# Cross attention: square sums of the eight head pairs in one burst at the end of a block, in four column groups

## The chip, the core and the metric

One core of one Trainium2 chip runs the kernel as a single launch. The metric is device time in microseconds (us), median over the executions. A core has five engines that run their own instruction lists and meet at semaphores: TensorE (PE; its weight loads are listed as PEld), VectorE (DVE), ScalarE (ACT), GpSimd (POOL) and SyncE (SP), which here only starts DMAs. Matmul results land in PSUM, eight banks of 128 partitions x 512 float32.

## What is computed

The program is one decoder layer in float32: a gated delta attention, a cross attention over 77 context tokens, and a mixture of 8 experts. The change lies in the cross attention alone. In the terms of the reference (its set-up calls the pieces `L0_xattn`):

```python
# 4 sequences x 1024 tokens x 256; 16 heads of 64; context (4, 77, 256)
def rms_norm(x, w):
    var = jnp.mean(jnp.square(x), axis=-1, keepdims=True)
    return x * jax.lax.rsqrt(var + EPS) * w          # over each head's 64 numbers
# q = rms_norm(x1 @ Wq per head), k = rms_norm(ctx @ Wk per head), v = ctx @ Wv
# out = softmax(q k^T, masked) v, heads side by side, @ Wo, added to x1, then a layer norm
```

The norm of the query needs one number for each token and head: the square root of the sum of the 64 squares of that head's query. The kernel does not scale the query with it. It keeps the reciprocal (`rq`) and gives it to the exponential as its scale.

## The kernel before

`build` runs the stages one after another with a barrier between them: `project_stage`, `delta_stage`, `context_stage`, `cross_stage`, `route_stage`, `expert_stage`, `final_stage`. The change is in `cross_stage` (and in the table of constants).

`cross_stage` takes the 4096 tokens in eight blocks of 512 (`BLK` = 4 tiles of 128). The function `blocks` calls `turn` once for each block on every engine: turn 0, a loop of three that holds turns 1 to 6, and turn 7. The work in a turn is software pipelined: turn n attends with block n while it makes the queries of block n+1. The 16 heads go in eight pairs (`XJ` = 8, 128 numbers each), and a step j of a turn handles one pair. On PE a step is: `scores(j+1)` (L1343), `queries(n+1, j)` (L1294), `square_sums(n+1, j-1)` (L1302), `weights_turned(j)` (transposes of the softmax weights, L1355), `values(j-1)` (L1364), and in some steps the turned output (L1320) or router logits (L1328) of the block before. There is no scheduler: each engine does exactly what stands in its `turn`, in that order, and waits with `wait_ge` on semaphores.

What the other engines do in a step:

- DVE: `masked(j+1)`: adds the mask to the scores out of PSUM (L1523, two instructions), takes the maximum (L1526), makes the bias `nb` (L1530). Then `normed(j)`: reciprocal of the softmax sums (L1535) and the scaling of the weights (L1537), which is what `weights_turned(j)` waits for. Then a copy of turned weights (L1549).
- ACT: copies the query pair out of PSUM (`query_out`, L1423), eight exponentials (L1450), copies of turned weights (L1471) and of the values' result (L1458).
- POOL: squares the query pair into `q2` (L1265), and nothing else.

The square sums: before, `q2` is a pair of buffers of one head pair each. For each pair j PE multiplies the squares by a column of ones for each of its two heads (the constant table from `C_HEAD`, 16 columns per pair) and accumulates all eight pairs into the same 16 rows of PSUM bank `SS` (`start` at j = 0, `stop` at j = 7), so `SS` holds heads x tokens. At the end of the turn ACT takes the square root into `ss` (`sums_out`, L1431), PE transposes it to tokens x heads (`sums_turned`, L1309, into bank `X`), and DVE takes the reciprocal into `rq` (L1494), as the last thing of its turn. PE's `x1_turned(n+1)` (L1286) at the start of the next turn waits for `rq_done`, because it writes over bank `X`.

The end of a turn on PE, in order: `values(7)`, `square_sums(n+1, 7)`, the output projection (64 matmul records of 256 columns, L1393), `sums_turned`, then the next turn's `scores(0)`, `x1_turned`, `scores(1)`, `queries(0)`. A float32 matmul of 512 columns shows in the trace as two weight loads and two matmul records.

Of the kernel before, what the change touches and what calls it, by code (L numbers as in the profile page):

```python
# [7 lines left out]
P = 128  # L8
F32 = mybir.dt.float32
I32 = mybir.dt.int32  # L10
ALU = mybir.AluOpType
ACT = mybir.ActivationFunctionType
# [5 lines left out]
BLK = 4  # L18
BT = BLK * P
# [12 lines left out]
XH, XD, CTX = 16, 64, 77  # L32
XW = XH * XD
# [7 lines left out]
C_ID, C_LE, C_GT, C_GE, C_ONE = 0, P, 2 * P, 3 * P, 4 * P  # L41
# [6 lines left out]
C_COL = C_IOTA + P  # L48
C_LOW = C_COL + 1
C_HEAD = C_LOW + NE * NE  # L50
C_N = C_HEAD + XW // P * XH


def constants():

    p, j = np.arange(P)[:, None], np.arange(P)[None, :]
    c = np.zeros((P, C_N), np.float32)
    c[:, C_ID:C_ID + P] = p == j
    c[:, C_LE:C_LE + P] = p <= j
    c[:, C_GT:C_GT + P] = p > j  # L60
    c[:, C_GE:C_GE + P] = p >= j
    c[:, C_ONE:C_ONE + P] = 1
    c[:, C_NM0:C_NM0 + P] = -1.0 * ((p // 2 == j // 2) & (p % 2 == 0) & (j % 2 == 1))
    for lev in range(1, LEVELS):
        s = 2 ** lev
        m = (p // (2 * s) == j // (2 * s)) & (p % (2 * s) >= s) & (j % (2 * s) < s)
        c[:, C_LEV + (lev - 1) * P // 2:C_LEV + lev * P // 2] = m[:, (np.arange(P) % (2 * s)) < s]
    c[:, C_BLK:C_BLK + 2] = p // XD == np.arange(2)[None, :]
    c[:, C_LT:C_LT + P] = p < j
    c[:, C_IOTA:C_IOTA + P] = j  # L70
    c[:, C_COL:C_COL + 1] = p
    e = np.arange(NE)
    c[:, C_LOW:C_HEAD] = (e[None, :] < e[:, None]).reshape(1, -1)
    for j in range(XW // P):
        c[:, C_HEAD + j * XH:C_HEAD + (j + 1) * XH] = np.arange(XH)[None, :] == 2 * j + p // XD
    return c


# [1047 lines left out]
def cross_stage(nc, a, s):  # L1126
# [7 lines left out]
    with ExitStack() as ctx:  # L1134
        sb = lambda n, shape: ctx.enter_context(nc.sbuf_tensor(n, shape, F32))
        bank = lambda n: ctx.enter_context(nc.psum_tensor(n, [P, 512], F32))
        sem = ctx.enter_context(stage_semaphores(nc))
        T, R, W = range(BLK), range(2), range(BLK // 2)
        XJ = XW // P
        two = lambda n, shape: [sb(f"{n}{k}", shape) for k in R]  # L1140
# [3 lines left out]
        con = s["con"]  # L1144
# [4 lines left out]
        eps = sb("eps4", [P, 2])  # L1149
# [4 lines left out]
        madd = sb("madd4", [P, CTX])  # L1154
        x1T = sb("x1T", [P, KD, BT])
        qT = two("qT", [P, XJ, BT])
        q2 = two("q2_", [P, BT])
        ss = sb("ss4", [XH, BT])
        rq = sb("rq", [P, BLK, XH])
        sc = two("sc", [P, BLK, 2, CTX])  # L1160
        mx = two("mx", [P, BLK, 2])
# [12 lines left out]
        V, Q, SS, X = bank("xV"), bank("xQ"), bank("xSS"), bank("xX")  # L1174
        weights_in = sem("x_weights_in")
        wo_in = sem("x_wo_in")
        q2_done = [sem(f"x_q2_done{k}") for k in R]
        ss_done = [sem(f"x_ss_done{k}") for k in R]
        names = ("set_up xq_in xr_in kv_in zero_out x2_out lg_out x1T_done x1T_sb q_done q_sb ss_sb ss_seen ssT_done "
                 "rq_done sc_done added mx_done nb_done exp_done den_done scaled tr_done tr_a tr_b pv_done o_sb "  # L1180
                 "wo_done y_done st_done st_seen mv_done sd_done r_done x2_done x2T_done x2T_sb lg_done lg_sb").split()
        (set_up, xq_in, xr_in, kv_in, zero_out, x2_out, lg_out, x1T_done, x1T_sb, q_done, q_sb, ss_sb, ss_seen, ssT_done,
         rq_done, sc_done, added, mx_done, nb_done, exp_done, den_done, scaled, tr_done, tr_a, tr_b, pv_done, o_sb,
         wo_done, y_done, st_done, st_seen, mv_done, sd_done, r_done, x2_done, x2T_done, x2T_sb, lg_done, lg_sb) = [
            sem(f"x_{n}") for n in names]
# [1 line left out]
        ident = con[:, C_ID:C_ID + P]  # L1187
        HX = XJ // 2
# [60 lines left out]
        @block.gpsimd  # L1249
        def _(pool):  # L1250
            nc.gpsimd.memset(eps[:, 0:1], EPS).then_inc(set_up, 1)
            nc.gpsimd.memset(eps[:, 1:2], XD * EPS).then_inc(set_up, 1)

            for k in R:
                nc.gpsimd.memset(empty[k][:], 0.0).then_inc(set_up, 1)
            pool.wait_ge(set_up, 4)
            for k in R:
                nc.gpsimd.tensor_scalar(empty[k][:, D + 1:ROW], con[:, C_COL:C_COL + 1], float((2 * TILES + k) * P), None,
                                        ALU.add).then_inc(set_up, 1)

            def squares(m, b):
                for j in range(XJ):
                    pool.wait_ge(q_sb, m * XJ + j + 1)
                    pool.wait_ge(ss_done[j % 2], m * HX + j // 2)
                    nc.gpsimd.tensor_tensor(q2[j % 2][:], qT[b][:, j, :], qT[b][:, j, :], ALU.mult  # L1265
                                            ).then_inc(q2_done[j % 2], 1)

            def turn(n, i, half, first, last):
                if not last:
                    squares(n + 1, 1 - half)  # L1270

            squares(0, 0)
            blocks(pool, turn)

        @block.tensor
        def _(pe):
# [17 lines left out]
                    mm = pe.matmul(Q[:], w_q[:, c, j * P:(j + 1) * P], x1T[:, c, :], start=c == 0, stop=c == KD - 1)  # L1294
                mm.then_inc(q_done, 1)

            def square_sums(m, j):

                pe.wait_ge(q2_done[j % 2], m * HX + j // 2 + 1)
                if j == 0:  # L1300
                    pe.wait_ge(ss_sb, m)
                pe.matmul(SS[0:XH, :], con[:, C_HEAD + j * XH:C_HEAD + (j + 1) * XH], q2[j % 2][:], start=j == 0,  # L1302
                          stop=j == XJ - 1).then_inc(ss_done[j % 2], 1)

            def sums_turned(m):
                pe.wait_ge(ss_sb, m + 1)
                nc.tensor.sem_inc(ss_seen, 1)
                for t in T:
                    mm = pe.transpose(X[:, t * XH:(t + 1) * XH], ss[:, t * P:(t + 1) * P],  # L1309
                                      con[0:XH, C_ID:C_ID + XH])  # L1310
                mm.then_inc(ssT_done, 1)

            def x2_turned(n, k):
# [18 lines left out]
            def turn(n, i, half, first, last):  # L1332
                at = lambda j: n * XJ + j + 1
# [37 lines left out]
                for j in range(XJ):  # L1371
                    if j < XJ - 1:
                        scores(j + 1)
                    if not last:
                        queries(n + 1, j)
                        if j:
                            square_sums(n + 1, j - 1)
                    weights_turned(j)
                    if j:
                        values(j - 1)  # L1380
                    if not first and j in (X2T_STEP, X2T_STEP + 1):
                        x2_turned(n - 1, j - X2T_STEP)
                    if not first and j == LG_STEP:
                        logits(n - 1)
                values(XJ - 1)
                if not last:
                    square_sums(n + 1, XJ - 1)
                pe.wait_ge(o_sb, at(XJ - 1))
                pe.wait_ge(tr_a, at(XJ - 1))
                pe.wait_ge(tr_b, at(XJ - 1))  # L1390
# [10 lines left out]
            x1_turned(0, True)  # L1401
            for j in range(XJ):
                queries(0, j)
                if j:
                    square_sums(0, j - 1)
            square_sums(0, XJ - 1)
            sums_turned(0)
            pe.wait_ge(wo_in, 16 * 3)
            blocks(pe, turn)
# [5 lines left out]
        def _(act):  # L1415
# [7 lines left out]
                nc.scalar.activation(qT[b][:, j, :], Q[:], ACT.Copy).then_inc(q_sb, 1)  # L1423

            def sums_out(m):
                act.wait_ge(ss_done[0], m * HX + HX)
                act.wait_ge(ss_done[1], m * HX + HX)
                if not (isinstance(m, int) and m == 0):
                    act.wait_ge(ssT_done, m)

                nc.scalar.activation(ss[:], SS[0:XH, :], ACT.Sqrt, bias=eps[0:XH, 1:2]).then_inc(ss_sb, 1)  # L1431

            def x2_sd(n):
                act.wait_ge(mv_done, n + 1)
# [56 lines left out]
        def _(dve):  # L1491
            def sums_out(m):
                dve.wait_ge(ssT_done, m + 1)
                nc.vector.reciprocal(rq[:], X[:, 0:BLK * XH].rearrange("p (t h) -> p t h", t=BLK)  # L1494
                                     ).then_inc(rq_done, 1)

            def norm(n):
                dve.wait_ge(sd_done, n + 1)
# [13 lines left out]
            def turn(n, i, half, first, last):  # L1512
                at = lambda j: n * XJ + j + 1

                def masked(j):

                    dve.wait_ge(sc_done, at(j))
                    if j == 0:
                        dve.wait_ge(kv_in, i * 48 + 48)
                    mask = madd[:].unsqueeze(1).unsqueeze(1).broadcast_to([P, 2, 2, CTX])  # L1520
                    for k in W:
                        pairs = S[k][:, 0:4 * KC].rearrange("p (t r c) -> p t r c", t=2, r=2)[:, :, :, 0:CTX]
                        m = nc.vector.tensor_tensor(sc[j % 2][:, 2 * k:2 * k + 2], pairs, mask, ALU.add)  # L1523
                    m.then_inc(added, 1)
                    dve.wait_ge(added, at(j))
                    nc.vector.tensor_reduce(mx[j % 2][:], sc[j % 2][:], AX_X, ALU.max).then_inc(mx_done, 1)  # L1526
                    if j == 0:
                        dve.wait_ge(rq_done, n + 1)
                    dve.wait_ge(mx_done, at(j))
                    nc.vector.scalar_tensor_tensor(nb[j % 2][:], mx[j % 2][:], -1.0, rq[:, :, 2 * j:2 * j + 2],  # L1530
                                                   ALU.mult, ALU.mult).then_inc(nb_done, 1)
# [599 lines left out]
```

## Time and profile before

| | us |
|---|---|
| median of three executions | 2601.34 |
| lowest and highest of the three | 2521.79, 2608.93 |
| profiled execution, its own time | 2520.27 |
| its span | 2518.6 |
| cross stage in it (first query to last router logits, by PE's timeline) | about 1221 to 1894 |

Of the span, PE is busy 1986.6 us (79%), PE's weight loads 1405.6, DVE 1223.3 (49%), ACT 952.5 (38%), POOL 470.9 (19%). A busy share is an average over seven stages that have different limits, so the page's shares don't say what PE's time is worth in this stage. That has to be read from the order of time in it: at each point, which engine does the others wait for.

In the timelines below a row is: start in us from the span's start, length in us, engine, line, operation, tiles written and read, partitions or shape, how many instructions were merged into the row, and in brackets the engine's idle time ahead of it with what ended it. The start of one PE row to the start of the next is what the first one costs PE; the lengths of PE rows overlap the next row, since matmuls are pipelined.

### The profile page before, as it was taken

To read this page: it belongs to the slowest core of one execution; us is meant where nothing else is said; L and a number is where in the kernel's file an instruction comes from. 1 tells how busy PE (TensorE), PEld (TensorE's weight loads), DVE (VectorE), ACT (ScalarE), POOL (GpSimd) and SP (SyncE) were. 2 spreads that over 40 slices of the span, in tenths; PEclk is the share of its full clock that TensorE was granted. 3 is DMA by queue.
4 is the path that set the end of the run, shared out by engine and by line. 5 is a ranking of instruction groups with operands and counts; after the bars stand their busy time and mean duration, and the time that the engine had idled before them with its cause. 6 is when DMAs were issued, how large, how long until landed. Compare 5 with 4: busy or idle time off the path is not lost. (4 is left out here: it accounts for less than half of the span.)

```text
span 2518.6 us, 35861 instructions
## 1 busy us (share of the span) xinstructions
PE 1986.6 (79%) x10951; PEld 1405.6 (56%) x10952; DVE 1223.3 (49%) x2673; ACT 952.5 (38%) x2558; POOL 470.9 (19%) x486
## 2 busy tenths in 40 slices
PE   6999578979879789796588889988771079999980
PEld 3444267968869678683245555555550046666650
DVE  5999744544554445553044444454334034444447
ACT  4777423233232332333265555666430022222220
POOL 1222231120220202201111111111002612222220
PEclk9999789989989899898789999999765589999995
DMA  2333341120211211202950100001007531111116
GB/s 72 117 117 117 114 119 51 34 84 17 67 50 51 67 30 54 74 9 68 237 189 26 42 26 33 9 25 41 17 5 230 167 111 45 45 44 46 46 40 200
DMA packets 147699, 184.86 MB, mean 73 GB/s; under 512 B 35267, under 2 KB 107383, under 8 KB 147519
## 3 DMA queue, kind: packets, MB, share of 16 engines
q1 hardware_dynamic: 122719, 145.45, 19.1%
q0 software_dynamic: 10288, 22.04, 2.5%
q10 hardware_dynamic: 14640, 16.78, 2.0%
q8 instruction: 20, 0.33, 0.1%
q14 instruction: 32, 0.26, 0.0%
HBM read 114.74 MB, written 69.49 MB: 73 GB/s over the span
## 5 line engine op out<-in xcount | busy, mean ns | idle before, releaser
L1450 ACT ACTIVATE sc<-sc,nb,rq 128x77 f32<-128x77 f32 x512 | 223.1, 440 | 25.0 <-DVE nb L1530 24.9
L1918 ACT ACTIVATE xsT<-pX 128x256 f32<-128x256 f32 x72 | 27.7, 384 | 429.6 <-PE pX L1859 429.6
L812 ACT ACTIVATE U<-psAB 128x512 f32<-128x512 f32 x160 | 82.6, 602 | 274.2 <-PE psAB L743 274.2
L725 PE MATMUL psAB<-T,PB 128*128 128x64 f32 x1536 | 178.8, 275 | 0.0
L725 PEld LDWEIGHTS psAB<-T,PB 128*128 128x128 f32 x1536 | 178.1, 194 | 0.0
L513 DVE SCALAR_TENSOR_TENSOR conv_y<-conv_in,taps,conv_y 128x512 f32<-128x512 f32 x192 | 165.3, 876 | 20.3 <-ACT conv_y L384 15.8
L1265 POOL TENSOR_TENSOR q<-qT 128x512 f32<-128x512 f32 x64 | 78.6, 1229 | 485.7 <-ACT qT L1423 485.7
L733 PE MATMUL psAB<-Z,U 128*128 128x64 f32 x1280 | 149.4, 275 | 0.0
L870 DVE TENSOR_TENSOR Z<-psAB,con 128x256 f32<-128x256 f32 x192 | 81.5, 425 | 136.2 <-PE psAB L725 136.2
L733 PEld LDWEIGHTS psAB<-Z,U 128*128 128x128 f32 x1280 | 146.2, 192 | 0.0
L1874 PE MATMUL pG<-w_gu,xsT 128*128 x284 | 135.4, 600 | 1.3 <-ACT xsT L1918 1.1
L1891 PE MATMUL pD<-w_d,hT 128*128 x568 | 134.2, 379 | 0.0
L1874 PE MATMUL pU<-w_gu,xsT 128*128 x284 | 133.4, 592 | 0.0
L1294 PE MATMUL xQ<-x1T,xw_q 128*128 128x512 f32 x256 | 131.2, 637 | 2.6 <-ACT x1T L1419 1.2
L1955 DVE TENSOR_TENSOR g<-pG,b_gu 128x512 f32<-128x512 f32 x71 | 49.1, 691 | 170.1 <-PE pU L1874 170.1
L309 PE MATMUL ps_j<-xnT,w_qkv 128*128 128x512 f32 x256 | 131.6, 651 | 0.0
L1835 POOL DMA_INDIRECT y<-o,idx x71 | 71.0, 1000 | 312.8 <-DVE o L1977 312.8
L1355 PEld LDWEIGHTS xT<-con,sc 128*77 128x77 f32 x512 | 63.8, 164 | 113.4 <-DVE sc L1537 92.0
L1355 PE MATMUL xT<-con,sc 128*77 128x128 f32 x512 | 80.4, 307 | 59.2 <-DVE sc L1537 59.0
L679 POOL DMA_DIRECT2D x<-x1t x32 | 17.8, 556 | 574.9 <-DVE x1t L947 573.8
L1859 PE MATMUL pX<-con,xs 128*128 128x128 f32 x144 | 27.8, 275 | 112.5 <-DMA xs<-xs 112.5
L1393 PE MATMUL xT<-xw_o,oT 128*128 128x256 f32 x512 | 112.6, 381 | 0.7 <-ACT oT L1458 0.7
(275 smaller groups left out, 4006.8 us busy)
## 6 DMA issues: line engine op xcount, KB each, us to landing
qkvg<-tok SPq DMA_DIRECT2D x8, 2048.0 KB, 6.6
xs<-empty SPq DMA_DIRECT2D x2, 4644.0 KB
step<-step SPq DMA_DIRECT2D x36, 256.0 KB, 4.6
qk<-qkvg SPq DMA_DIRECT2D x36, 256.0 KB, 5.2
xs<-xs SPq DMA_DIRECT2D x72, 128.0 KB, 2.0
qkvg<-gate SPq DMA_DIRECT2D x8, 1024.0 KB, 8.8
vb<-qkvg SPq DMA_DIRECT2D x32, 256.0 KB, 3.7
gt<-qkvg SPq DMA_DIRECT2D x32, 256.0 KB, 2.6
```

The lines of the kernel that those rows point to most:

```text
L309: mm = pe.matmul(ps_j[j % 2][:], w_qkv[:, c, j * P:(j + 1) * P], xnT[b][:, c, :], start=c == 0, stop=c == KD - 1)
L513: y = nc.vector.scalar_tensor_tensor(conv_y[m % 4][:], conv_in[b][:, m, k:k + BT], taps[:, m, k:k + 1], conv_y[m % 4][:], ALU.mult, ALU.add)
L725: mm = pe.matmul(A[b][:, k * HP:(k + 1) * HP], PB[b][:, k, 1, :], T[b][:, k, :].rearrange("p (m w j) -> p m w j", w=2, j=2 ** lev)[:, :, 0 ...
L733: mm = pe.matmul(B[b][:, k * HP:(k + 1) * HP], U[b][:, k, :], Z[b][:, k, :], start=True, stop=True)
L812: nc.scalar.activation(flat(U[b]), A[b], ACT.Copy).then_inc(lev_xs, 1)
L870: nc.vector.tensor_tensor(Z[b][:], A[b][:, 0:H * HP].rearrange("p (k j) -> p k j", k=H), con[:, m:m + HP].unsqueeze(1).broadcast_to([P, H, ...
L1294: mm = pe.matmul(Q[:], w_q[:, c, j * P:(j + 1) * P], x1T[:, c, :], start=c == 0, stop=c == KD - 1)
L1355: mm = pe.transpose(TB[r][0:CTX, t * P:(t + 1) * P], sc[j % 2][:, t, r, :], ident)
L1393: mm = pe.matmul(TB[t // 2][:, (t % 2) * D:(t % 2 + 1) * D], oT[:, j, t * P:(t + 1) * P], w_o[:, j, :], start=j == 0, stop=j == XJ - 1)
L1450: e = nc.scalar.activation(sc[j % 2][:, t, r, :], sc[j % 2][:, t, r, :], ACT.Exp, bias=nb[j % 2][:, t, r:r + 1], scale=rq[:, t, 2 * j + r: ...
L1874: mm = pe.matmul(bk[:], xsT[q][:, c, :], w_gu[:, bass.ds(e, 1), c, k * FF:(k + 1) * FF], start=c == 0, stop=c == KD - 1)
L1891: mm = pe.matmul(pD[q][:, 0:D], hT[q][:, k, :], w_d[:, bass.ds(e, 1), k, :], start=k == 0, stop=k == FK - 1)
```

## The change

The eight square sums of a block are no longer taken pair by pair in the steps. POOL writes the squares of all eight pairs into one larger tile `q2` (128 x 8 x 512). PE does nothing with them until the end of the turn. There, `square_sums(m)` issues the eight matmuls back to back. Pair j goes to column group j mod 4 of the array (`tile_position=(0, 32*(j % 4))`), with 32 columns of weights, and writes the 32 rows of `SS` of that group: pairs 0 to 3 with `start`, pairs 4 to 7 accumulated on top with `stop`. The result fills all 128 rows of `SS`, four useful rows in each group of 32. So the square root is taken over 128 rows in place of 16, the four transposes are of 128 x 128 in place of 16 x 128, and the reciprocal picks the useful columns with two instructions of 32 numbers a partition, in place of one of 64. Semaphores `q2_done` and `ss_done` become one each, and `rq_half` is added. The constant table is 64 columns narrower.

```diff
-C_N = C_HEAD + XW // P * XH
+C_N = C_HEAD + 2 * 32
...
-    for j in range(XW // P):
-        c[:, C_HEAD + j * XH:C_HEAD + (j + 1) * XH] = np.arange(XH)[None, :] == 2 * j + p // XD
+    for k in range(2):
+        c[:, C_HEAD + 32 * k:C_HEAD + 32 * k + 32] = np.arange(32)[None, :] == 2 * k + p // XD
...
-        q2 = two("q2_", [P, BT])
-        ss = sb("ss4", [XH, BT])
+        q2 = sb("q2_", [P, XJ, BT])
+        ss = sb("ss4", [P, BT])
...
-                    pool.wait_ge(ss_done[j % 2], m * HX + j // 2)
-                    nc.gpsimd.tensor_tensor(q2[j % 2][:], qT[b][:, j, :], qT[b][:, j, :], ALU.mult
-                                            ).then_inc(q2_done[j % 2], 1)
+                    if j == 0:
+                        pool.wait_ge(ss_done, m)
+                    nc.gpsimd.tensor_tensor(q2[:, j, :], qT[b][:, j, :], qT[b][:, j, :], ALU.mult
+                                            ).then_inc(q2_done, 1)
...
-            def square_sums(m, j):
-
-                pe.wait_ge(q2_done[j % 2], m * HX + j // 2 + 1)
-                if j == 0:
-                    pe.wait_ge(ss_sb, m)
-                pe.matmul(SS[0:XH, :], con[:, C_HEAD + j * XH:C_HEAD + (j + 1) * XH], q2[j % 2][:], start=j == 0,
-                          stop=j == XJ - 1).then_inc(ss_done[j % 2], 1)
+            def square_sums(m):
+
+                pe.wait_ge(q2_done, m * XJ + XJ)
+                pe.wait_ge(ss_sb, m)
+                for j in range(XJ):
+                    k, at = j // 4, 32 * (j % 4)
+                    mm = pe.matmul(SS[at:at + 32, :], con[:, C_HEAD + 32 * k:C_HEAD + 32 * k + 32], q2[:, j, :],
+                                   start=k == 0, stop=k == 1, tile_position=(0, at))
+                mm.then_inc(ss_done, 1)
...
-                    mm = pe.transpose(X[:, t * XH:(t + 1) * XH], ss[:, t * P:(t + 1) * P],
-                                      con[0:XH, C_ID:C_ID + XH])
+                    mm = pe.transpose(X[:, t * P:(t + 1) * P], ss[:, t * P:(t + 1) * P], ident)
...
                         queries(n + 1, j)
-                        if j:
-                            square_sums(n + 1, j - 1)
                     weights_turned(j)
...
                 values(XJ - 1)
                 if not last:
-                    square_sums(n + 1, XJ - 1)
+                    square_sums(n + 1)
...
-                nc.scalar.activation(ss[:], SS[0:XH, :], ACT.Sqrt, bias=eps[0:XH, 1:2]).then_inc(ss_sb, 1)
+                nc.scalar.activation(ss[:], SS[:], ACT.Sqrt, bias=eps[:, 1:2]).then_inc(ss_sb, 1)
...
-                nc.vector.reciprocal(rq[:], X[:, 0:BLK * XH].rearrange("p (t h) -> p t h", t=BLK)
-                                     ).then_inc(rq_done, 1)
+                sums = X[:].rearrange("p (t g i) -> p t g i", t=BLK, i=32)
+                for k in range(2):
+                    nc.vector.reciprocal(rq[:, :, 8 * k:8 * k + 8].rearrange("p t (g r) -> p t g r", r=2),
+                                         sums[:, :, :, 2 * k:2 * k + 2]).then_inc((rq_half, rq_done)[k], 1)
```

The instruction order of PE in steps 6 and 7 and at the end of turn 0, before the change. `xQ` are the queries, `xSS` the square sums (`q_0` and `q_1` are the two buffers of squares), `xT` with `sc` the turned weights, `xV` the values, `xT` with `xw_o` the output projection, `xX` with `ss` the turned sums.

```order
L1343 MATMUL xS<-kT,qT 128x156 x4
L1294 MATMUL xQ<-x1T,xw_q 128x512 x2
L1302 MATMUL xSS<-q_1,con 16x512
L1355 MATMUL xT<-con,sc 77x128 x8
L1364 MATMUL xV<-aT,v 64x512 x2
L1294 MATMUL xQ<-x1T,xw_q 128x512 x2
L1302 MATMUL xSS<-q_0,con 16x512
L1355 MATMUL xT<-con,sc 77x128 x8
L1364 MATMUL xV<-aT,v 64x512 x4
L1302 MATMUL xSS<-q_1,con 16x512
L1393 MATMUL xT<-xw_o,oT 128x256 x32
L1309 MATMUL xX<-con,ss 128x16 x4
```

The same place in the changed kernel:

```order
L1343 MATMUL xS<-kT,qT 128x156 x4
L1293 MATMUL xQ<-x1T,xw_q 128x512 x2
L1355 MATMUL xT<-con,sc 77x128 x8
L1364 MATMUL xV<-aT,v 64x512 x2
L1293 MATMUL xQ<-x1T,xw_q 128x512 x2
L1355 MATMUL xT<-con,sc 77x128 x8
L1364 MATMUL xV<-aT,v 64x512 x4
L1302 MATMUL xSS<-q_,con 32x512 x8
L1391 MATMUL xT<-xw_o,oT 128x256 x32
L1310 MATMUL xX<-con,ss 128x128 x4
```

The square sum between the queries and the turned weights is gone from each step, and the eight of them stand between the last values and the output projection, where one stood. The transposes of the sums behind the projection are 128 columns wide in place of 16. On DVE the end of turn 0, first before and then after:

```order
L1556 TENSOR_TENSOR x2t<-xr,xT 128x512
L1561 BN_STATS stats<-x2t 128x6 x2
L1565 BN_AGGR mv<-stats 128x2 x4
L1494 RECIPROCAL rq<-xX 128x64
```

```order
L1554 TENSOR_TENSOR x2t<-xr,xT 128x512
L1559 BN_STATS stats<-x2t 128x6 x2
L1563 BN_AGGR mv<-stats 128x2 x4
L1491 RECIPROCAL rq<-xX 128x4x8 x2
```

The place of the reciprocal in DVE's order is the same; it is two instructions in place of one.

## Rows read from the trace of the kernel before

**Rows 1.** Stretches: us, busy PE, PEld, DVE, ACT, POOL; clock, DMA, GB/s. Turns 2, 7.

```profile
1417.00:1493.00 76.00, 68.18 (x310) 40.32 (x308) 33.76 (x79) 46.08 (x160) 9.90 (x8) 0.98 0.07 22
1804.00:1864.00 60.00, 42.41 (x150) 29.41 (x148) 22.50 (x49) 30.66 (x118) 0.00 (x0) 0.53 0.03 9
```

**Rows 2.** Timeline of PE in turn 2, step 4 and the start of step 5.

```profile
1452.70 1.10 PE L1355 MATMUL xT<-con,sc 128*77 128x128 f32 x8 [0.25 <-DVE sc L1537]
...
1454.74 1.33 PE L1343 MATMUL xS<-kT,qT 128*128 128x156 f32 x8
1455.90 1.88 PE L1294 MATMUL xQ<-x1T,xw_q 128*128 128x512 f32 x4
1457.71 1.03 PE L1302 MATMUL xSS<-q,con 128*16 128x512 f32 x2
1458.99 1.10 PE L1355 MATMUL xT<-con,sc 128*77 128x128 f32 x8 [0.25 <-DVE sc L1537]
```

**Rows 3.** Timeline of DVE over the same time.

```profile
1456.10 0.86 DVE L1523 TENSOR_TENSOR sc<-xS,madd 128x308 f32<-128x308 f32 x2 [1.58 <-PE xS L1343]
...
1458.14 0.80 DVE L1537 TENSOR_TENSOR sc<-sc,den 128x616 f32<-128x616 f32 x1
```

**Rows 4.** Step 1 of the same turn, PE, and DVE's scaling.

```profile
1431.74 0.80 DVE L1537 TENSOR_TENSOR sc<-sc,den 128x616 f32<-128x616 f32 x1
...
1433.02 1.10 PE L1355 MATMUL xT<-con,sc 128*77 128x128 f32 x8
```

**Rows 5.** Timeline of PE, step 7 and the end of the turn.

```profile
1471.03 1.03 PE L1302 MATMUL xSS<-q,con 128*16 128x512 f32 x2
1471.99 1.10 PE L1355 MATMUL xT<-con,sc 128*77 128x128 f32 x8
...
1474.80 1.08 PE L1364 MATMUL xV<-aT,v 77*64 77x512 f32 x4 [0.70 <-ACT oT L1458]
1475.81 1.03 PE L1302 MATMUL xSS<-q,con 128*16 128x512 f32 x2
1476.77 14.08 PE L1393 MATMUL xT<-xw_o,oT 128*128 128x256 f32 x64
1490.78 0.42 PE L1309 MATMUL xX<-con,ss 16*128 16x16 f32 x4
```

**Rows 6.** The same turn: POOL's last squares, DVE at step 7 and at the end.

```profile
1471.81 1.04 POOL L1265 TENSOR_TENSOR q<-qT 128x512 f32<-128x512 f32 x1 [3.89 <-ACT qT L1423]
...
1470.24 0.80 DVE L1537 TENSOR_TENSOR sc<-sc,den 128x616 f32<-128x616 f32 x1
...
1492.81 0.52 DVE L1494 RECIPROCAL rq<-xX 128x64 f32<-128x64 f32 x1
```

**Rows 7.** PE's first transposes of the next turn, and their wait.

```profile
1493.48 0.63 PE L1286 MATMUL xQ<-con,xq 128*128 128x128 f32 x4 [1.02 <-DVE rq L1494]
```

**Rows 8.** Groups by line and shape: busy us, mean ns, then idle before.

```profile
L1302 PE MATMUL xSS<-q,con 128*16 128x512 f32 x128 | 66.4, 600 | 0.8 <-POOL q L1265 0.8
L1535 DVE RECIPROCAL den<-den 128x8 f32<-128x8 f32 x64 | 12.6, 197 | 31.0 <-ACT sc L1450 31.0
L1494 DVE RECIPROCAL rq<-xX 128x64 f32<-128x64 f32 x8 | 4.2, 528 | 54.2 <-PE xX L1309 54.2
```

**Rows 9.** Timeline of PE: the first block's queries, turn 0's wait, turn 7.

```profile
1225.12 3.78 PE L1294 MATMUL xQ<-x1T,xw_q 128*128 128x512 f32 x4 [0.69 <-ACT qT L1423]
...
1267.92 1.12 PE L1286 MATMUL xQ<-con,xq 128*128 128x128 f32 x4 [15.95 <-DMA xq<-x]
...
1811.83 1.98 PE L1364 MATMUL xV<-aT,v 77*64 77x512 f32 x4
1813.73 2.45 PE L1343 MATMUL xS<-kT,qT 128*128 128x156 f32 x8
1819.11 1.99 PE L1355 MATMUL xT<-con,sc 128*77 128x128 f32 x8 [2.93 <-DVE sc L1537]
```

**Rows 10.** Stretch from the start of turn 3's transposes, columns as in Rows 1.

```profile
1494.00:1499.00 5.00, 3.59 (x17) 2.04 (x15) 2.98 (x7) 4.39 (x13) 0.00 (x0) 1.00 0.52 175
```

More of the change, by code:

```diff
@@ L1176, in cross_stage @@
         wo_in = sem("x_wo_in")
-        q2_done = [sem(f"x_q2_done{k}") for k in R]
-        ss_done = [sem(f"x_ss_done{k}") for k in R]
-        names = ("set_up xq_in xr_in kv_in zero_out x2_out lg_out x1T_done x1T_sb q_done q_sb ss_sb ss_seen ssT_done "
+        names = ("q2_done ss_done rq_half set_up xq_in xr_in kv_in zero_out x2_out lg_out x1T_done x1T_sb q_done q_sb ss_sb ss_seen ssT_done "
                  "rq_done sc_done added mx_done nb_done exp_done den_done scaled tr_done tr_a tr_b pv_done o_sb "
                  "wo_done y_done st_done st_seen mv_done sd_done r_done x2_done x2T_done x2T_sb lg_done lg_sb").split()
-        (set_up, xq_in, xr_in, kv_in, zero_out, x2_out, lg_out, x1T_done, x1T_sb, q_done, q_sb, ss_sb, ss_seen, ssT_done,
+        (q2_done, ss_done, rq_half, set_up, xq_in, xr_in, kv_in, zero_out, x2_out, lg_out, x1T_done, x1T_sb, q_done, q_sb, ss_sb, ss_seen, ssT_done,
          rq_done, sc_done, added, mx_done, nb_done, exp_done, den_done, scaled, tr_done, tr_a, tr_b, pv_done, o_sb,
@@ L1403, in _ @@
                 queries(0, j)
-                if j:
-                    square_sums(0, j - 1)
-            square_sums(0, XJ - 1)
+            square_sums(0)
             sums_turned(0)
@@ L1425, in sums_out @@
             def sums_out(m):
-                act.wait_ge(ss_done[0], m * HX + HX)
-                act.wait_ge(ss_done[1], m * HX + HX)
+                act.wait_ge(ss_done, m + 1)
                 if not (isinstance(m, int) and m == 0):
                     act.wait_ge(ssT_done, m)
-                nc.scalar.activation(ss[:], SS[0:XH, :], ACT.Sqrt, bias=eps[0:XH, 1:2]).then_inc(ss_sb, 1)
+                nc.scalar.activation(ss[:], SS[:], ACT.Sqrt, bias=eps[:, 1:2]).then_inc(ss_sb, 1)
             def x2_sd(n):
@@ L1527, in masked @@
                     if j == 0:
+                        dve.wait_ge(rq_half, n + 1)
                         dve.wait_ge(rq_done, n + 1)
```

## The prediction

> **What bounds the kernel now.** The page gives PE 79% of the span, so it is tempting to price a matmul saved on PE at its own length. I read the stretches first [rows 1]: an inner turn of the cross stage takes some 75 us, PE is busy 68.2 us of a 76 us stretch, ACT 46.1, DVE 33.8, at a granted clock of 0.98. PE is nearly full, but not alone on the path, and the timelines show where.
>
> In a middle step [rows 2] PE starts `scores(j+1)` at 1454.74, the queries at 1455.90, the square sum at 1457.71 and the turned weights at 1458.99. Ahead of the last stands 0.25 us of idle time that DVE's scaling ended. DVE [rows 3] starts on those scores at 1456.10 and ends the scaling at 1458.14 + 0.80 = 1458.94, which is what releases PE at 1458.99. So from the scores to the turned weights the time is set by the chain scores, DVE's mask, maximum, bias, sum and scaling, and PE's queries and square sum lie beside it. A square sum costs PE 0.96 us (1475.81 to 1476.77 in [rows 5]). It is cover, and the chain ends 0.3 us after it. One whole step takes 1458.99 - 1452.70 = 6.29 us.
>
> Outside the steady steps PE does set the time. In step 1 DVE has scaled by 1431.74 + 0.80 = 1432.54, and PE turns the weights only at 1433.02 [rows 4]. In step 7, which has no next scores, DVE has scaled at 1470.24 + 0.80 = 1471.04 [rows 6], and PE does the square sum from 1471.03 and turns the weights at 1471.99 [rows 5]. From there on PE is the path to the output projection at 1476.77, which runs 14.01 us without a break. At the end DVE's batch norm and reciprocal set the time: PE's next transposes have waited 1.02 us for `rq` [rows 7].
>
> **The change part by part, for one inner turn.**
>
> *The square sums of steps 2 to 6 (five of them) go.* PE would be ready at 1457.71 in place of 1458.67, but DVE's chain still ends at 1458.94. Nothing is late that was early: gain 0, and PE's wait of 0.25 us grows to about 1.25 us. The upper bound of a gain would be 0.96 each, if the wait didn't take the place.
>
> *The one of step 1 goes.* PE could turn the weights just behind DVE's 1432.54, with the same 0.05 us that lies between 1458.94 and 1458.99, at 1432.59: 0.43 us sooner. That step ran while the clock was just rising, and turns differ in it, so the bounds are 0 and -0.43; I take -0.2, the middle.
>
> *The one of step 7 goes.* The turned weights start at 1471.09 in place of 1471.99: -0.90 us. Everything behind them that PE does moves with them, the values of pairs 6 and 7 too. The last values start at 1473.90 and take 1.01 us to issue (1474.80 to 1475.81), so the burst can start at 1474.91. POOL's eighth square ends at 1471.81 + 1.04 = 1472.85 [rows 6], so the wait for all eight is no wait.
>
> *The burst.* The trace has no group of four in the array, but it has one of two: `values` gives two heads 64 columns each, four records of 512 columns, and the pair costs 1.01 us [rows 5], where one square sum alone, two records of 512 columns, costs 0.96. Two matmuls in different column groups thus run side by side. If four do as two do, a round of four costs 1.01 and the burst of two rounds 2.02 us, and the projection starts at 1474.91 + 2.02 = 1476.93 in place of 1476.77: +0.16 together with step 7. The lower bound is set by ACT: the projection also waits for the copy of the last values, 0.70 us behind their end as in the wait ahead of 1474.80, so it can't start before about 1475.7: -1.1. The upper bound is eight square sums in a row as now, 8 x 0.96 = 7.68 us, which puts the projection at 1482.59: +5.82. Two at a time would be 4 x 1.01 = 4.04: +2.18. I take 2.02, since the row of the pair is the only one with column groups.
> The Trainium skill, TensorE: Matmul & The Clock Gate, section Measured speedup vs the span model, has three column groups of 32 at 2.38 times the speed of one after another, not 3 times. By that figure the burst would be an estimated 7.68 / 2.38 = 3.2 us, 1.2 us a turn over the pair's row and about 8 us in all; the trace's pair is 1.92 / 1.01 = 1.9 times of 2.
> The Trainium skill, TensorEngine Tiling (Array Packing), section Key Properties, says that changing the tiling mode drains the array, which speaks against a burst between 64 column and full width work. The trace has such changes already ([rows 5]: two groups of 64 columns at 1474.80, one matmul of 16 at 1475.81, the whole width at 1476.77), and their price, if any, is inside the costs of 1.01 and 0.96 us.
>
> *Behind the burst.* The square root over 128 rows and ACT's other work there lie under 14.01 us of projection. The four transposes are as wide as those of [rows 7], 0.63 in place of 0.42 us [rows 5]: +0.21, hidden, because DVE takes the reciprocal only at 1492.81 and they end at 1491.20 [rows 5, 6]. The reciprocal is on the path [rows 7]. A reciprocal of 8 numbers takes 197 ns and one of 64 takes 528 [rows 8], or 5.9 ns a number, so 32 numbers take about 339 and two of them 678 ns: +0.15 us. The bounds are -0.13 (2 x 197 less 528) and +0.53 (2 x 528). DVE's `masked(0)` waits behind them in its queue, and PE's `x1_turned` for them; both are late by the same 0.15.
>
> *The first block and the ends.* The first block's squares come before turn 0, and there PE waits 15.95 us for a load a little later [rows 9], so a burst of any of these lengths is covered. Turn 7 makes no queries. So seven turns count, 0 to 6. POOL does the same eight multiplications; PE waited 0.8 us in all for it in 128 records [rows 8]. No DMA moves on any queue; the table of constants is 64 columns smaller.
>
> **The sum.** A turn: 0 (steps 2 to 6) - 0.2 (step 1) + 0.16 (step 7 and burst) + 0.15 (reciprocal) = +0.11 us, times 7 = +0.8 us. Against the profiled execution, 2520.27, that is 2521.1. That execution stands beside the lowest of the three runs shown (2521.79), while the median is 2601.34 and the highest 2608.93. Nothing in the profile says what adds 80 us to a run, and the change does not touch a cause that I can see. Put on the median, the sum is 2602. Both levels have to be in the range.
>
> **Rivals.**
> (a) *The groups run only two at a time, or overlap worse than the pair.* For it: no row has four. Against: the pair's row, at nearly full overlap. 7 x (2.18 + 0.15 - 0.2) = +15 us, 2616.
> (b) *The groups run one after another.* 7 x (5.82 - 0.05) = +40 us, 1.6%: 2642. It is past 2% only if something else comes on top, such as the clock falling during a burst that uses a quarter of the array.
> (c) *Slower, by the clock.* The new idle time, 1.25 us in each step, could let the granted clock drop to its lower level, 1.2 GHz. For it: in turn 7, which has neither queries nor squares, PE waits 2.93 us for DVE in a step and the stretch's clock is 0.53 [rows 1, 9]. Against: after the 1.02 us wait of [rows 7] came transposes and scores, and the next 5 us, PE busy 3.59, ran at 1.00 [rows 10]. Price: at the lower level a step's PE work is 1.99 (weights turned) + 1.90 (values) + 2.45 (scores) + 3.78 (queries, 1.88 in [rows 2]) = 10.1 us [rows 9], against 6.29: +3.8 for each such step. It decides from 52 / 3.8 = 14 of the 35 steps; all 35 would be +133 us, 2735.
> (d) *Faster, because PE does set the steps.* If all six early square sums came off the path, 7 x 6 x 0.96 = -40 us, 2561, still inside 2%. Against it stands the bracket of [rows 2] and DVE's end 0.05 us ahead of it. With the steps at the full clock it would have to come with less time lost to the lower clock at the start of each turn to pass 2%.
>
> **How the numbers follow.** The forecast, a change of a few us at most, 0.68. (a) 0.12, (b) 0.08, (c) 0.06, (d) 0.02, and 0.04 that the two levels of the run times fall unevenly on the two kernels. Faster by over 2%: half of the last and half of (d), 0.03. Slower: most of (c), a quarter of (b) and half of the last, 0.08. Within 2%: 0.89. Two per cent is about what a measurement of this kernel can tell from no change. The likeliest case alone is 2510 to 2614: its own bounds, 7 x -1.66 = -12 us (-0.43, -1.1, -0.13) and 7 x +0.7 = +5 us (0, +0.16, +0.53), on the lowest and the highest of the runs shown. With (a) on the upper level, 2608.93 + 15, the range is 2510 to 2625; (b), most of (c) and part of the rest stay out.
>
> **What would show it.** In the profile after: the turned weights wait about 1.25 us for DVE's scaling in the steady steps and a step still takes 6.3 us; the projection starts about 3.0 us behind the start of the last values (1.97 before); the burst's sixteen records start in groups of four, and the projection 2.0 us behind the first of them; two reciprocals of about 340 ns; turns of 75 us at a clock of 0.96 to 0.98. It is wrong if the records of the burst start 0.43 us apart one after another, if the steady steps get shorter than 6.2 us, or if the clock of an inner turn falls under 0.9.

## The result and the profile after

| us | before | changed |
|---|---|---|
| median of four executions | 2564.61 | 2602.78 |
| the four | 2521.79, 2527.87, 2601.34, 2608.93 | 2598.84, 2600.01, 2605.54, 2607.01 |
| profiled execution, span | 2518.6 | 2604.0 |
| granted clock over the span | 0.888 | 0.853 |

The comparison gives a ratio of 1.0309 (1.027 to 1.0348), slower. It cannot be understood without one fact: the executions of this program lie on two levels, and the ratio sets the changed kernel's four against those of before near 2525 alone. The forecast of 2602 us was hit as a time, and that was luck: the sum of +0.8 us was put on a median that happened to lie on the upper level, and so did all four executions of the changed kernel. The forecast "no change" was missed as a ratio, and the question is what the 3% are.

The page after:

```profile
span 2604.0 us, 35785 instructions
...
PE 2028.4 (78%) x10951; PEld 1483.1 (57%) x10952; DVE 1222.9 (47%) x2681; ACT 955.0 (37%) x2558; POOL 473.3 (18%) x486
```

PE is busy 42 us longer than before although it has the same number of records. Busy time in stretches, here of the kernel before: the delta stage, and the cross stage's turns 0 to 6 (columns as in [rows 1]).

```profile
345.00:1147.00 802.00, 694.12 (x5883) 642.53 (x5881) 397.18 (x1012) 237.25 (x645) 129.47 (x146) 0.94 0.17 49
...
1250.70:1796.20 545.50, 480.29 (x2141) 286.65 (x2140) 231.13 (x506) 321.29 (x1117) 70.31 (x56) 0.95 0.16 49
```

The same two stretches of the changed kernel:

```profile
345.00:1227.50 882.50, 780.74 (x5885) 723.73 (x5884) 396.29 (x1009) 240.36 (x645) 129.61 (x146) 0.83 0.15 44
...
1333.30:1876.10 542.80, 436.40 (x2140) 281.71 (x2139) 231.02 (x512) 321.35 (x1117) 71.66 (x56) 0.96 0.16 49
```

The delta stage, in which not a line was changed, takes the same 5,880 records of PE in about 80 us more, at a granted clock of 0.83 in place of 0.94. The seven turns, where the change is, take 542.8 in place of 545.5 us. So the 85 us of the spans are +82.6 by the start of the first reciprocal (1333.32 against 1250.74; 80.5 of them in the delta stage's stretch, 2.1 between it and the reciprocal), -2.6 in the turns, and 5.4 behind them.

Where the two traces part can be seen to the microsecond. PE ahead of the delta stage's first merges (L725, L733: narrow matmuls of 64 columns, each with a weight load of 128), and the stretch behind their start. The kernel before, its timeline and then the busy time and clock:

```profile
342.36 3.16 PE L714 MATMUL psAB<-con,U 128*128 128x128 f32 x12 [1.01 <-DVE U L864]
345.31 3.83 PE L725 MATMUL psAB<-T,PB 128*128 128x64 f32 x32
```

```profile
346.00:363.50 17.50, 17.50 (x161) 17.50 (x160) 7.91 (x17) 3.67 (x9) 4.16 (x4) 1.00 0.49 123
```

The changed kernel, the same two views:

```profile
343.93 2.13 PE L714 MATMUL psAB<-con,U 128*128 128x128 f32 x8 [0.19 <-DVE U L864]
345.86 6.93 PE L725 MATMUL psAB<-T,PB 128*128 128x64 f32 x32
```

```profile
346.00:363.50 17.50, 17.50 (x85) 17.50 (x84) 3.39 (x8) 2.83 (x5) 4.16 (x4) 0.50 0.47 123
```

Up to here both executions do the same instructions within 1.1 us of each other, and the first PE record of the stage starts at 321.47 in both. In both the clock falls to 1.2 GHz a few microseconds ahead of the merges. But before, it is back at 2.4 GHz 0.3 us after they have begun, and after, it stays at 1.2 GHz: 161 matmul records in 17.5 us against 85. PE is busy without a gap in both. The same fork comes in every one of the stage's eight rounds. In a later round of the changed kernel, its timeline, then the busy time and clock of two stretches:

```profile
570.62 6.93 PE L725 MATMUL psAB<-T,PB 128*128 128x64 f32 x32
577.35 7.03 PE L733 MATMUL psAB<-Z,U 128*128 128x64 f32 x32
584.17 3.62 PE L743 MATMUL psAB<-con,T 128*128 128x128 f32 x16
```

```profile
570.70:589.00 18.30, 18.30 (x89) 18.30 (x88) 3.39 (x8) 2.99 (x5) 4.17 (x5) 0.50 0.41 117
589.00:620.00 31.00, 31.00 (x281) 31.00 (x281) 15.68 (x32) 6.20 (x12) 0.00 (x0) 1.00 0.00 0
```

The first merge of this round took 3.95 and 3.73 us before (at 549.85 and 553.64) and takes 6.93 and 7.03 here, and only some 18 us into the round's merges the clock is granted again.

Which of the two comes goes with where the clock falls against the merges. In a late round of the kernel before (merges from 959.42) and one of the changed kernel (merges from 1021.08):

```profile
955.00:956.50 1.50, 0.48 (x5) 0.25 (x3) 1.50 (x2) 0.60 (x1) 1.50 (x2) 1.00 0.00 0
956.60:960.00 3.40, 3.40 (x16) 2.72 (x16) 1.85 (x2) 1.53 (x3) 2.90 (x4) 0.50 0.00 0
960.10:970.00 9.90, 9.90 (x92) 9.90 (x91) 3.79 (x9) 2.22 (x5) 2.08 (x3) 1.00 0.79 184
```

```profile
1017.60:1019.10 1.50, 0.66 (x4) 0.42 (x4) 1.50 (x3) 0.43 (x2) 1.50 (x2) 1.00 0.00 0
1019.10:1039.50 20.40, 20.35 (x96) 20.04 (x96) 4.41 (x9) 3.91 (x7) 6.23 (x7) 0.50 0.43 105
```

The clock falls 2.8 us ahead of the merges before, and the time until it comes back is nearly all transposes; in the changed kernel it falls 2.0 us ahead, and the merges take up most of what follows.

The cross stage of the changed kernel, by contrast, is what the forecast drew. PE in step 4 of turn 2:

```profile
1535.48 1.10 PE L1355 MATMUL xT<-con,sc 128*77 128x128 f32 x8 [1.22 <-DVE sc L1535]
...
1537.52 1.33 PE L1343 MATMUL xS<-kT,qT 128*128 128x156 f32 x8
1538.68 1.88 PE L1293 MATMUL xQ<-x1T,xw_q 128*128 128x512 f32 x4
1541.78 1.10 PE L1355 MATMUL xT<-con,sc 128*77 128x128 f32 x8 [1.21 <-DVE sc L1535]
```

The end of the turn, PE and then DVE's reciprocals:

```profile
1553.88 1.10 PE L1355 MATMUL xT<-con,sc 128*77 128x128 f32 x8
...
1556.68 1.08 PE L1364 MATMUL xV<-aT,v 77*64 77x512 f32 x4 [0.70 <-ACT oT L1453]
1557.69 1.92 PE L1302 MATMUL xSS<-q_,con 128*32 128x512 f32 x16
1559.55 14.08 PE L1391 MATMUL xT<-xw_o,oT 128*128 128x256 f32 x64
1573.46 0.60 PE L1310 MATMUL xX<-con,ss 128*128 128x128 f32 x4
```

```profile
1575.59 0.54 DVE L1491 RECIPROCAL rq<-xX 128x32 f32<-128x32 f32 x2
```

The step still takes 6.30 us, with 1.22 us of waiting for DVE where 0.25 stood [rows 2]. The burst of all eight pairs costs 1.86 us.

### The profile page after: what moved, and what is told of

Same layout as the page of the kernel before. It is cut to its first block and busy times, and to the rows that moved or that the text cites. A ratio compares the mean times of both kernels' runs of the same rounds, so it can differ in the third digit from the quotient of the medians.

```text
span 2604.0 us, 35785 instructions
## 1 busy us (share of the span) xinstructions
PE 2028.4 (78%) x10951; PEld 1483.1 (57%) x10952; DVE 1222.9 (47%) x2681; ACT 955.0 (37%) x2558; POOL 473.3 (18%) x486
## 5 line engine op out<-in xcount | busy, mean ns | idle before, releaser
L725 PE MATMUL psAB<-T,PB 128*128 128x64 f32 x1536 | 208.1, 301 | 0.0
L725 PEld LDWEIGHTS psAB<-T,PB 128*128 128x128 f32 x1536 | 207.9, 221 | 0.0
L733 PE MATMUL psAB<-Z,U 128*128 128x64 f32 x1280 | 175.8, 304 | 0.0
L733 PEld LDWEIGHTS psAB<-Z,U 128*128 128x128 f32 x1280 | 172.5, 220 | 0.0
L1264 POOL TENSOR_TENSOR q_<-qT 128x512 f32<-128x512 f32 x64 | 80.0, 1250 | 481.3 <-ACT qT L1419 481.3
L881 DVE TENSOR_TENSOR T<-T,psAB 128x256 f32<-128x256 f32 x160 | 67.5, 422 | 101.4 <-PE psAB L733 101.4
```

The source lines that it names most:

```text
L725: mm = pe.matmul(A[b][:, k * HP:(k + 1) * HP], PB[b][:, k, 1, :], T[b][:, k, :].rearrange("p (m w j) -> p m w j", w=2, j=2 ** lev)[:, :, 0 ...
L733: mm = pe.matmul(B[b][:, k * HP:(k + 1) * HP], U[b][:, k, :], Z[b][:, k, :], start=True, stop=True)
L1264: nc.gpsimd.tensor_tensor(q2[:, j, :], qT[b][:, j, :], qT[b][:, j, :], ALU.mult).then_inc(q2_done, 1)
```

## The experiments

Two theories. C, chance: the delta stage has two steady patterns of the clock, an execution falls into one or the other whatever the kernel, and the change is worth nothing. K: something in the change puts the delta stage into the long pattern, or makes the kernel slower itself.

**The kernels again.** `a_again` and `a_third` are the changed kernel, `b_again` the kernel before, all without an edit.

> The changed kernel once more. In its first profile the delta stage, whose code is the same in both kernels, took 82 us longer than before, with the granted clock at its lower level for eleven stretches of 3.4 us in each of its 8 rounds in place of four; the cross stage's seven turns took 2.6 us less. Theory C (chance): the delta stage has two steady patterns of the clock, about 82 us apart, and which one an execution falls into hangs on when the program starts against the clock's own changes. Then some of the executions here come out near 2520 and others near 2600. Theory K (the change does it): some part of the change, such as the narrower table of constants or the moved addresses, puts every execution into the longer pattern; then all come out between 2595 and 2610.

> The kernel before, unchanged, timed against itself. Theory C: the same two levels, near 2520 and near 2603, as often as for the changed kernel, so that even this pair may differ by up to 3%. Theory K: mostly near 2520 or evenly split, and clearly more often low than the changed kernel.

> The changed kernel once more, to count its executions on each level. So far 1 of 10 of the changed kernel came out near 2525, and 10 of 33 of the kernel before. Theory C: 1 to 3 of the six here come out low. Theory K in its weaker form (the change makes the long pattern likelier): again 0 or 1 of 6.

Measured: `a_again` 2526.41 once and five from 2601.15 to 2608.36; `a_third` 2522.22, 2527.80 and four from 2598.25 to 2607.22; `b_again` 2525.41, 2525.75, 2527.34 and three from 2603.56 to 2607.0. The profiles of `a_again` and `a_third` fell on the short pattern. `a_third`, the changed kernel, in the two stretches shown of before:

```profile
346.00:363.50 17.50, 17.50 (x160) 17.50 (x160) 7.91 (x17) 3.57 (x8) 4.16 (x4) 1.00 0.49 123
...
345.00:1147.00 802.00, 694.36 (x5882) 642.64 (x5880) 397.18 (x1012) 236.91 (x644) 129.05 (x146) 0.94 0.16 49
```

That is the delta stage of the first profile of before, to 0.3 us of PE's busy time, in the changed kernel. No profile of the kernel before fell on the upper level; that its executions there are of the same kind is read from their times and from their mean clock, 0.851 to 0.856, where the changed kernel's upper ones have 0.852 to 0.858. Over all runs the kernel before has 43 executions, 11 of them on the low level (2517.09 to 2535.66, mean 2524.5) and 32 on the high one (2605.1). The changed kernel has 16: 3 low (2525.5) and 13 high (2604.5). On each level the two kernels agree within 1 us. At 11 in 43 one would look for 4 low ones in 16, so 3 say nothing of a difference. The strong form of K (always long) has fallen; that the change moves the odds a little can't be ruled out with these numbers, and nothing speaks for it.

**The table of constants.**

```diff
-C_N = C_HEAD + 2 * 32
+C_N = C_HEAD + XW // P * XH
```

> The changed kernel with the table of constants padded to its old width of 1603 columns, so that the first loads and all addresses ahead of the cross stage are those of before. If the narrower table puts the delta stage in the longer pattern (a form of theory K), this falls back to the split of before, with runs near 2520. Theory C: the same split as the changed kernel's.

Measured: 2522.79 once and five from 2601.28 to 2609.13, the same split as the changed kernel's. One low of six is too few to tell this split from that of before. But the changed kernel runs low with its narrow table too (`a_again`, `a_third`), so its loads and addresses do not force the long pattern.

**Without the delta stage.**

```diff
-        delta_stage(nc, a, s)
+        copy_stage(nc, a, s)
```

`copy_stage` is one DMA that copies `x` to `x1`, so all that follows does the same instructions on other numbers.

> The kernel before without its delta stage: x1 is a copy of x, so everything behind works on other numbers, with the same instructions. It takes the stage with the two clock patterns out, so the cross stage can be read alone. Both theories: about 2520 - 905 = 1620 us, and no second level 80 us higher. If a second level stays, the pattern isn't the delta stage's alone.

> The changed kernel without its delta stage (x1 is a copy of x), to be compared with the same of before. Theory C (the change is worth nothing in itself, the 3% came from the delta stage's two patterns): within 5 us of it, likeliest 1 to 3 us shorter, as the seven turns took 2.6 us less in the first profile. Theory K (the change itself slows the kernel): tens of us longer here too.

Measured, six executions each: before 1691.49 to 1702.81, mean 1697.5; changed 1691.52 to 1702.76, mean 1697.7. Two numbers of mine were off here: the time is 1698 and not 1620, since I had the stage's share at 905 us and it is some 827 (2524.5 less 1697.5), and the changed kernel is not 1 to 3 us shorter but 0.2 longer, with a standard error of 2.6. What decides is that the second level is gone and with it the 3%: the whole change, alone, is worth nothing that twelve executions can tell.

**The move without the column groups.** `q2` as in the change, the eight matmuls in a burst, but each of 16 columns into the same 16 rows as before. Once with the delta stage (`b_move`), once without (`m_nodelta`).

```diff
                         queries(n + 1, j)
-                        if j:
-                            square_sums(n + 1, j - 1)
...
                 if not last:
-                    square_sums(n + 1, XJ - 1)
+                    for j in range(XJ):
+                        square_sums(n + 1, j)
```

> The kernel before with only the move: all eight square sums in a burst at the end of a turn, each still 16 columns wide into the same 16 rows, with the large tile of squares. My sum's bound for groups that run one after another: the burst takes 8 x 0.96 = 7.7 us, a turn of the cross stage gets about 5.8 us longer than the changed kernel's 75.0, and the seven turns 40 us. Whole time 40 us over the changed kernel on the same level of the delta stage (about 2560 or 2640). Rival: the burst overlaps with itself anyway, since one group follows another, and costs under 4 us; then under +20 us.

> The move alone (eight square sums in a burst, all into the same 16 rows), without the delta stage. By the sum, 7 turns x 5.8 us = 40 us over the same of the changed kernel. With the pattern of the delta stage gone this should stand out of the noise. The rival that a longer burst is partly covered gives under 30 us.

Measured: `b_move` 2558.01 to 2567.51 (three) and 2638.22 to 2643.64 (three), means 2563.1 and 2641.8, which is +38.6 and +36.7 us on the two levels of before. `m_nodelta` 1735.1, +37.4 on the changed kernel (standard error 2.5). So the two levels are there too, and the move by itself costs 37 to 39 us: the column groups only pay back what the burst costs without them. PE's timeline of `m_nodelta` at the end of a turn:

```profile
579.97 1.08 PE L1377 MATMUL xV<-aT,v 77*64 77x512 f32 x4 [0.70 <-ACT oT L1469]
580.98 7.04 PE L1315 MATMUL xSS<-q_,con 128*16 128x512 f32 x16
587.95 14.08 PE L1405 MATMUL xT<-xw_o,oT 128*128 128x256 f32 x64
```

Sixteen records here too, with weights 16 columns wide in place of 32, and 6.97 us against 1.86: four column groups run 3.7 times as fast as none.

**Seven of the eight square sums left out**, without the delta stage. Only the last pair's is taken, with `start` and `stop`; the squares of the other seven pairs are in no sum. The semaphore counts are changed to match.

```diff
-                if j == 0:
-                    pe.wait_ge(ss_sb, m)
-                pe.matmul(SS[0:XH, :], con[:, C_HEAD + j * XH:C_HEAD + (j + 1) * XH], q2[j % 2][:], start=j == 0,
-                          stop=j == XJ - 1).then_inc(ss_done[j % 2], 1)
+                pe.wait_ge(ss_sb, m)
+                pe.matmul(SS[0:XH, :], con[:, C_HEAD + j * XH:C_HEAD + (j + 1) * XH], q2[j % 2][:], start=True,
+                          stop=True).then_inc(ss_done[j % 2], 1)
...
                         queries(n + 1, j)
-                        if j:
-                            square_sums(n + 1, j - 1)
```

> The kernel before without its delta stage and without seven of the eight square sums of a block (only the last pair's is taken, so the norms are wrong). My sum: the five of the steady steps are worth nothing, that of step 1 0 to 0.43 us, that of step 7 0.9 us, so seven turns get 6 to 9 us shorter. Rival d (PE sets the steps): 7 x 7 x 0.96 = 47 us shorter.

Measured: 1693.4, 4.1 us under before, with a standard error of 2.7. That is a little under my 6 to 9, within the noise of them (and, at 1.5 standard errors, not clearly apart from nothing), and it excludes the 47 of the rival in which PE sets the steps. In its trace the wait stands in the place of the square sum, and a step takes 6.3 us:

```profile
537.61 1.10 PE L1368 MATMUL xT<-con,sc 128*77 128x128 f32 x8 [1.22 <-DVE sc L1545]
...
641.01 1.10 PE L1368 MATMUL xT<-con,sc 128*77 128x128 f32 x8 [1.22 <-DVE sc L1545]
...
645.03 1.10 PE L1368 MATMUL xT<-con,sc 128*77 128x128 f32 x8
```

The last two rows are steps 6 and 7 of the next turn. They lie 4.02 us apart where it was 4.91 before (1467.08 to 1471.99), so step 7 gives the 0.90 us that I had given it, and PE has no wait there. It is so in six of the seven turns; in the other the clock fell in step 6, and a wait of 0.50 us for DVE took back part of the gain.

**Filler in the delta stage**, to test what makes the two patterns, and to be rid of the long one. Behind each of the four groups of transposes ahead of the first merge (`FILL` is 2, and 1 in `b_fill1`):

```diff
                         mm = pe.transpose(A[b][:, k * P:(k + 1) * P], U[b][:, k, :], ident)
                     mm.then_inc(y0_done, 1)
+                    for _ in range(FILL):
+                        pe.matmul(B[b][:, 2 * P:4 * P], ident, PB[b][:, 0, :, :].rearrange("p w j -> p (w j)"),
+                                  start=True, stop=True)
```

> The kernel before with filler in the delta stage: behind each of the four groups of transposes that come ahead of the first merge (where PE waits for VectorE anyway), two float32 matmuls of 256 columns into a part of PSUM that nobody reads then. In the long pattern the merges start at the lower clock and stay there for six stretches of 3.4 us; in the short one the clock is up for them. Theory C, and that PE's work just ahead of the merges decides which: all executions on one level, the short pattern plus the filler's own price of 0 to 3 us in each of 8 rounds, so 2520 to 2545. Rival: the pattern is decided elsewhere in the round; then both levels stay, each a little longer.

> The changed kernel with the same filler in the delta stage. Theory C: one level, within 5 us of the same of before, which makes the two kernels comparable at full length; the 80 us are gone from it too. Theory K (the change puts the stage in the long pattern): it stays near 2600 here, or well above the same of before.

> The kernel before with half of the filler (one matmul behind each group of transposes). If how much PE has done ahead of the merges decides, this may be enough for one level at a smaller price (2520 to 2535), or leave some executions on the upper one. If two matmuls each give one level and one doesn't, the amount is what counts.

Measured: `b_fill` 2530.15 to 2538.54, mean 2534.9; `a_fill` 2525.06 to 2538.08, mean 2532.9 (1.9 less, standard error 2.7); `b_fill1` 2533.30 to 2542.62, mean 2536.2. None of the eighteen executions is on the upper level, while the kernel before, timed beside them, was there nine times of ten. PE's timeline of `b_fill` in a round:

```profile
548.47 0.66 PE L717 MATMUL psAB<-con,U 128*128 128x128 f32 x4 [2.73 <-DVE U L870]
548.96 1.03 PE L720 MATMUL psAB<-PB,con 128*128 128x256 f32 x4
550.14 0.66 PE L717 MATMUL psAB<-con,U 128*128 128x128 f32 x4 [0.15 <-DVE U L870]
...
553.24 1.03 PE L720 MATMUL psAB<-PB,con 128*128 128x256 f32 x4
554.10 3.68 PE L731 MATMUL psAB<-T,PB 128*128 128x64 f32 x32
```

The filler fills the 1.01 us wait that PE had there and lengthens the rest by a little, and the merges start at the full clock in this round. It costs some 10 us against the low level (7 for the changed kernel) and gains 70 against the high one. Half of it is enough for the kernel before, but it is not the cheaper one that I had looked for: 2536.2. With it the clock still falls in every second round, 3.8 to 4.0 us ahead of the merges, and comes back before they begin. Matmuls put just ahead of the merges take the long pattern away; that is shown for both kernels. Whether it is their work that does it, or the 1 us by which they move the merges (5.63 us from the first transposes to the merges in the round above, 4.62 in the same round of before), is not separated. Both medians lie under those of the kernels without it, 2535 and 2535 against 2602 or so.

## Why the prediction was right or wrong

- *The steady steps are worth nothing (right).* The wait grew from 0.25 to 1.22 us, I had 1.25; the step is 6.30 us, I had 6.29. `n_nodelta` shows it without any burst.
- *The burst (right, slightly too dear).* 1.86 us for two rounds of four; the pair's row gave 2.02. The upper bound was too high as well: eight in a row cost 6.97 and not 7.68, so 0.87 us each where a lone one costs 0.96. The Trainium skill, TensorE: Matmul & The Clock Gate, section Measured speedup vs the span model, has 2.38 times for three groups. The estimate from it, 3.2 us, was farther off than the one from the trace's own pair.
- *The reciprocal (wrong in size).* Two of 32 numbers start to end in 0.54 us where one of 64 took 0.52, so +0.02 and not +0.15: the means of 312 ns overlap.
- *The transposes (right).* 0.60 us, hidden.
- *Step 7 (right) and step 1 (can't be told).* From step 6's turned weights to step 7's it is 4.02 us (1549.86 to 1553.88) in place of 4.91. The projection starts 2.87 us behind the start of the last values (1559.55 - 1556.68), I had 3.0; before it was 1.97, so the burst takes back the 0.90 of step 7 and no more. Step 1 moves with the clock's place in the turn: behind the turned weights of step 0 it took 6.41 to 7.61 us before, and from 5.98 (`a_third`) to 6.97 in the changed kernel, so my -0.2 can't be told.
- *The sum (right within the noise).* The seven turns come to 542.8 us against 545.5 in the first pair of profiles and to 545.55 in `a_third`; the sum said +0.8. Half a microsecond a turn is what the clock's own place in a turn moves. The experiments leave the sum of the change at 0 within 3 us: the two kernels differ by 1.0 and -0.6 us on the two levels, by 0.2 without the delta stage and by -1.9 with the filler, with standard errors of 2.3, 1.2, 2.6 and 2.7.
- *The two levels (the step that failed).* I wrote that nothing in the profile said what adds 80 us to a run, and gave 0.04 to the levels falling unevenly on the two kernels. Both were wrong. The runs show that the 80 us are the delta stage's: two patterns of the clock, 2524.5 against 2605.1 us on average, with 11 of 43 executions of one and the same kernel on the lower level. The page showed a granted clock of 0.888, and the delta stage showed it at 0.94 with the same falls in every round. I never looked at which matmuls run right behind such a fall, because the stage was not part of the change. And with three executions shown, two of them high, the odds that four of one kernel lie on one level and the comparison rests on that were far above one in twenty five: if one in four is low, four of four come out high about one time in three (0.75 to the fourth is 0.32), and with a low one of before already on the table that alone gives a ratio 3% up. My 0.08 for slower stood where 0.2 (from two of three high, as shown then) to 0.3 belonged.
- *Rival (c), the clock falling in the cross stage's steps.* It did not: 0.96 over the seven turns. The right resource, but the wrong stage: I looked for the clock only where the change was.

## What to carry to other kernels

Read a change's worth from the wait that ends last where it stands: here a wait for VectorE took the place of the five matmuls removed from the steady steps, and the column groups only paid back what the burst would have cost. Before you believe a ratio, take the two traces stage by stage, and if the time lies in a stage that the change doesn't touch, time the old kernel against itself and cut that stage out. A stage of narrow matmuls behind a short wait held the clock at half for 20 us on end in every round of the long pattern here; a few spare matmuls in that wait made it steady.

## What the runs showed of the hardware

- With TensorE's clock falling and rising, one and the same stage ran in one of two repeating patterns, rounds of 102.4 and of 112.6 us (the busy time of 88.36 us in a round of 102.4, 99.18 in one of 112.6):

```profile
520.00:622.40 102.40, 88.36 (x745) 81.44 (x744) 50.95 (x130) 30.58 (x83) 17.72 (x20) 0.93 0.18 52
```

```profile
540.00:652.60 112.60, 99.18 (x746) 91.64 (x746) 50.87 (x128) 30.88 (x83) 17.77 (x20) 0.83 0.16 47
```

- A PE without a gap between its records did not bring the clock back here: in 570.7 to 589.0 it was busy 18.30 of 18.30 us, mostly with matmuls of 64 columns and their weight loads, at 0.50 throughout.
- The pattern repeats itself by its place. In four profiles of the short pattern the clock falls 2.7 to 3.1 us ahead of the first merge in round 1 and 2.8 us ahead from round 4 on, and comes back 0.3 to 0.7 us into the merges. In three of the long one (`after`, `a_table`, `b_move`) it falls 2.6, 3.4 and 2.0 us ahead in round 1 and 2.0 us ahead from round 4 on, and stays down for 20.5 us. Both kernels are among the short ones.
- What sets that place in round 1 is not shown. The instructions were alike up to it, and what differed was when the clock changed: in the first stage, from 56.6 to 58.8 us, it stood at 1.00 in the first profile of before and at 0.50 in that of the changed kernel. But that is no key to the pattern: it stood at 0.55 there in `b_again`, which ran in the short one, and at 0.79 in `a_table`, which ran in the long one.
- Four column groups of 32 gave 3.7 times the rate of matmuls that all write the same 16 rows (6.97 against 1.86 us for eight float32 matmuls of 512 columns).
